# A two-layer graph network kernel: counting ahead of the messages, a second accumulator for the visits of the last four groups, and a ring of eight gathered quads

## The chip, the cores and the metric

The kernel runs on one core of a Trainium2 chip. The metric is the device time of one execution in microseconds (us). The engines are named as in the profile: PE is TensorE (PEld its weight load), DVE VectorE, ACT ScalarE, POOL GpSimd, SP SyncE.

## What is computed

There are 6,250 nodes with 128 features and 200,000 directed edges, sorted by target (`dst`). Both layers use the same edges; only the first uses the edges' 128 features.

```python
# layer 0, for each edge
m   = silu(concat(x[src], x[dst], e) @ msg_W1 + msg_b1) @ msg_W2 + msg_b2
agg = segment_sum(m, dst)
x1  = layernorm(x + layernorm0(x + mlp2(concat(x, agg))))
# layer 1
agg = segment_sum(x1[src], dst) / max(degree, 1)
out = layernorm(x1 + relu(relu(concat(x1, agg) @ W1 + b1) @ W2 + b2))
```

## The kernel before

**Units of work.** 128 edges are a tile, 4 tiles a quad (512 edges), 7 quads a group. There are 391 quads with edges in 56 groups (0 to 55), and the nodes are 49 blocks of 128. The edge stage is a loop over steps `s`; in each, every engine does its part of quad `s` or of a neighbour.

**The messages of layer 0.** POOL gathers the rows of the sources, four indirect DMAs a quad (L899), into a ring of nine quads (`gath`, `GS = 9`). Before those of quad `s` it waits until DVE's addition for quad `s - 9` is done. PE computes `ps_pre` (`products`, L1200 and L1207) for quad `s + 1`. DVE adds the gathered rows (`add`, L979, waits for `pre_mm`, `silu` and the gather). ACT applies silu (L1419). PE then sums over edges into the group's window of targets (`sums`, L1241 and L1243), for which it waits for `silu`. DVE adds a finished group's window to the accumulator `sumT` in SBUF (`add_sums`, L987).

**The counts for layer 1.** Layer 1's sum over sources needs, for each group, a matrix of how often each node is the source of each target of the group. It is counted by PE from one-hots of the edges. For quad `s + 1`, in step `s`, DVE makes the one-hots (`hots`: four of L964 and four of L966), PE multiplies them (`count`, eight of L1221 and two of L1227 that carry a column over), and in the next step ACT copies the counts out (`copy_counts`, L1363 and L1368). The integer keys of a group come from DVE (`make_keys`), and the finished matrix of a group goes to HBM in four parts (`store`, L1389) in the steps after its last quad. So counting runs one quad ahead of the sums and ends with them, in step 390.

**Visits.** Nodes' features after layer 0 (`x1`) are finished in 17 units of 2 to 4 blocks, as the sorted targets allow (`UNITS`, `unit_step`). A unit takes steps `s0` to `s0 + 9`, one small stage on one engine in most of them; the last one (blocks 46 to 48) starts at step 392, since it needs all messages. A visit `(s, d, lo, hi)` multiplies blocks `lo` to `hi` of `x1` with group `d`'s count matrix, which SP has loaded back (`load_visits`, L785), two matmuls for a block (L1257); DVE adds the 120 columns of the result to `sumT` (`add_visits`, L1012) one step later. `plan_visits` gives each step up to two visits of together at most 14 blocks (a bucket), four after step 391. A group can be visited from step `7(d + 1) + 9` on, since its matrix must be in HBM. Visits add to the same `sumT` as the messages' sums, whose columns are zeroed when their unit has been read (L1051), so a group whose window is not yet zeroed cannot be visited: groups 52 to 55 wait for the last unit. PE has two banks for visits, used in turn by buckets; a bucket waits until DVE has added the one before last.

**The tail.** From step 392 the last unit goes through its ten steps, the visits that are left are made, and 13 last units `w` (four blocks each) go through layer 1's update: POOL scales by the degree (L908), PE (L1317, L1319), ACT, PE (L1327, L1329), DVE, ACT, store. They follow the visits in an order set by `plan_last`.

PE in a step of before:

```python
products(s + 1); unit_step(s); visit(i) for i in VISITS_AT.get(s, ())
last_step(...); sums(s); count(s + 1)
```

## Time and profile before

| | us |
|---|---|
| median of 3 timed runs | 2902.84 (2895.51 to 2920.19) |
| profiled execution, its own time | 2885.56 |
| its span, first to last instruction | 2883.7 |
| first addition for a quad (step 0) to the last (step 390) | 85 to 2746.9 |
| from the last unit's first matmul to the end | 2753.25 to 2883.7 |

All busy times, stages and waits below are of the one profiled execution. The span is 1.9 us shorter than its time, and that time is 17.3 us below the median of the timed runs.

### The profile page before, as it was taken

How to read it: one execution, taken by the hardware profiler on the slowest of the kernel's cores; microseconds unless marked ns; L12 is line 12 of the kernel's file. 1: busy time of each engine (PE TensorE's matmuls, PEld its weight loads, DVE VectorE, ACT ScalarE, POOL GpSimd, SP SyncE). 2: the span in 40 equal slices, each digit the busy share in tenths (PEclk: the TensorE clock that was granted, in tenths of full speed). 3: DMA queues.
4: the chain of work that ended last, by engine and by line, in shares of the span. 5: the costliest groups of instructions: out<-in, count | busy, mean ns of one | idle time of the engine just before them, and what ended most of it. 6: DMA issues, size and time to landing. Idle time of an engine off the chain costs nothing.

```text
span 2883.7 us, 58406 instructions
## 1 busy us (share of the span) xinstructions
PE 2275.3 (79%) x19559; PEld 1944.8 (67%) x19559; DVE 1681.2 (58%) x5671; ACT 1475.2 (51%) x3771; POOL 1518.6 (53%) x1633
## 2 busy tenths in 40 slices
PE   5778777878787888777777778878888788887986
PEld 4666666666676766666666667767677676776874
DVE  5465655665555565565565656566555556555735
ACT  3454554555464554454555555455555454554614
POOL 5555556556555555555555555455554555554322
PEclk7776777877777876887888888888888888898998
DMA  6454555554555564555565555666565666666683
GB/s 218 121 153 142 148 152 152 160 150 150 162 155 154 153 175 142 177 166 169 152 182 164 174 173 176 185 167 182 165 187 173 174 193 173 186 173 192 200 296 97
DMA packets 305361, 487.72 MB, mean 169 GB/s; under 512 B 121342, under 2 KB 183944, under 8 KB 305056
## 3 DMA queue, kind: packets, MB, share of 16 engines
q10 hardware_dynamic: 94161, 245.05, 26.0%
q1 hardware_dynamic: 158895, 129.93, 16.4%
q0 software_dynamic: 52000, 108.96, 14.4%
q8 instruction: 158, 2.59, 0.4%
q14 instruction: 147, 1.20, 0.1%
HBM read 375.62 MB, written 108.13 MB: 168 GB/s over the span
## 4 chain that ended last, share of the span: by engine, by line
PE 48%; another core or an unknown queue 15%; issue 14%; DVE 10%; ACT 9%; ACTq 3%; DMA 1%; DVEq 0%; SPq 0%
PE ps_pre L1200 12%; PE ps_cnt L1221 11%; PE ps_l L1257 9%; PE ps_sum L1241 8%; DVE edgeK L966 4%; ACT counts L1363 3%; PE ps_pre L1207 3%; ACT farN L1399 2%; DVE edgeL L964 2%; ACT h L1419 1%; ACTq L1496 1%; PE ps_sum L1243 1%; DVE pre L979 1%; DVE nodeE L956 1%
## 5 line engine op out<-in xcount | busy, mean ns | idle before, releaser
L899 POOL DMA_INDIRECT gath<-P_d,src_i x1527 | 1444.3, 946 | 1185.4 <-DVE pre L979 748.0
L1200 PE MATMUL ps_pre<-wc,eT_c 128*128 128x128 f32 x3128 | 730.2, 354 | 61.7 <-issue 59.7
L1221 PE MATMUL ps_cnt<-edgeK,edgeL 128*128 128x250 bf16 (+1 forms) x3128 | 578.0, 338 | 197.8 <-ACT counts L1363 110.1
L1200 PEld LDWEIGHTS ps_pre<-wc,eT_c 128*128 128x128 f32 x3128 | 593.3, 234 | 119.6 <-issue 84.5
L966 DVE TENSOR_SCALAR edgeK<-iotaK,key 128x500 bf16<-128x500 f16 (+1 forms) x1564 | 667.7, 488 | 0.0
L979 DVE TENSOR_TENSOR pre<-ps_pre,gath 128x512 f32<-128x512 f32 x384 | 262.9, 685 | 686.5 <-remote 462.9
L1363 ACT ACTIVATE counts<-ps_cnt 128x1000 bf16<-128x1000 f32 x391 | 405.5, 1037 | 414.9 <-remote 228.2
L1241 PE MATMUL ps_sum<-edgeN,h 128*128 128x40 f32 x3128 | 481.5, 302 | 80.6 <-issue 68.9
L1221 PEld LDWEIGHTS ps_cnt<-edgeK,edgeL 128*128 128x128 bf16 x3128 | 319.0, 111 | 309.9 <-issue 210.3
L1241 PEld LDWEIGHTS ps_sum<-edgeN,h 128*128 128x128 f32 x3128 | 448.7, 217 | 101.2 <-issue 79.8
L1257 PE MATMUL ps_l<-A_v,x1h 128*128 128x120 bf16 x5020 | 359.7, 229 | 85.6 <-issue 74.6
L1207 PE MATMUL ps_pre<-Qw,nodeE 120*128 120x128 bf16 x1564 | 385.3, 246 | 38.9 <-issue 29.1
L1409 ACT ACTIVATE edgeN<-farN 128x160 f32<-128x160 f32 x391 | 127.9, 327 | 525.1 <-remote 435.0
L1399 ACT ACTIVATE farN<-iotaN,rel_g 128x40 f32<-128x40 f16 x1564 | 380.6, 314 | 29.9 <-issue 29.6
L1257 PEld LDWEIGHTS ps_l<-A_v,x1h 128*128 128x128 f16 x5020 | 315.3, 105 | 116.1 <-issue 101.1
L1419 ACT ACTIVATE h<-pre 128x512 f32<-128x512 f32 x391 | 243.2, 622 | 191.4 <-DVE pre L979 155.1
L964 DVE TENSOR_SCALAR edgeL<-iotaL,low 128x132 bf16<-128x132 f16 x1564 | 328.4, 272 | 0.0
L1012 DVE TENSOR_TENSOR sumT<-ps_l,sumT 128x120 f32 x443 | 123.6, 279 | 228.4 <-remote 154.6
L1207 PEld LDWEIGHTS ps_pre<-Qw,nodeE 120*128 120x128 bf16 x1564 | 181.2, 116 | 43.5 <-issue 33.7
L1243 PEld LDWEIGHTS ps_sum<-edgeB,onesb 128*128 128x128 bf16 x1564 | 118.3, 127 | 62.7 <-issue 62.7
L1243 PE MATMUL ps_sum<-edgeB,onesb 128*128 128x40 bf16 x1564 | 117.0, 188 | 52.3 <-issue 52.2
L956 DVE TENSOR_SCALAR nodeE<-rel_c,pidq 120x512 bf16<-120x512 bf16 x391 | 134.7, 345 | 2.4 <-DMA rel_c<-rel_d 2.4
(184 smaller groups left out, 1425.0 us busy)
## 6 DMA issues: line engine op xcount, KB each, us to landing
eT_c<-eT ACTq DMA_DIRECT2D x193, 512.0 KB
A_d<-counts ACTq DMA_DIRECT2D x168, 384.0 KB
rel_c<-rel_d ACTq DMA_DIRECT2D x193, 240.0 KB
A_v<-A_d SPq DMA_DIRECT2D x68, 448.0 KB
A_v<-A_d SPq DMA_DIRECT2D x97, 256.0 KB
gath<-P_d,src_i POOLq DMA_INDIRECT x1535
A_d<-counts ACTq DMA_DIRECT2D x56, 416.0 KB
A_v<-A_d SPq DMA_DIRECT2D x33, 384.0 KB
```

Of the source, the lines that this page charges most:

```text
L899: pool.indirect_dma_start(gath[:, r, t * D:(t + 1) * D], None, v["P_d"], bass.IndirectOffsetOnAxis(ap=src_i[g % RS][:, c:c + 1], axis=0)). ...
L964: V.tensor_scalar(edgeL[x][:, j, :], iotaL[:, :, 0:LC], low[k][:, q * QT + j:q * QT + j + 1], None, ALU.is_equal)
L966: last = V.tensor_scalar(edgeK[x][:, ROFF[j]:ROFF[j] + A2 * w], iotaK[j][:, :, 0:A2 * w // KR], key[k][:, q * QT + j:q * QT + j + 1], None ...
L979: V.tensor_tensor(pre[s % 2][:], ps_pre[s % 2][:], gath[:, s % GS, :], ALU.add).then_inc(pre_add, 1)
L1200: T.matmul(o, eT_c[c % RE][:, e0:e0 + P], wc[:], start=True, stop=False)
L1207: last = T.matmul(o, nodeE[x][:, t * P:(t + 1) * P], Qw[g % 2][:, q, :], start=False, stop=True)
L1221: last = T.matmul(o[:, :, w0:w0 + w], edgeL[x][:, j, 0:P], r, start=(j == 0), stop=(j == QT - 1 and q == 0), skip_group_check=True)
L1241: T.matmul(ps_sum[:, cols], h[x][:, t, :], edgeN[x][:, t, :], start=False, stop=True, skip_group_check=True)
L1257: last = T.matmul(l1_part(i), x1h[:, a, part, :], A[:, (a - lo) * P:(a - lo) * P + GW], start=(a == lo and part == 0), stop=(a == hi - 1 a ...
L1363: A.activation(counts[k][:].rearrange("p (b a) d -> p b a d", b=2)[:, :, :, bass.ds(off, W0)], ps_cnt[:, :, 0:AB * W0].rearrange("p b (a d ...
L1399: last = A.activation(farN[:, j, :], iotaN[:, q, :, 0:WN // KR], ACT.Square, scale=-1.0, bias=rel_g[k][:, q * QT + j:q * QT + j + 1])
L1419: A.activation(h[x][:, :, 0:D], pre[x][:].rearrange("p (t n) -> p t n", n=D), ACT.Silu).then_inc(silu, 1)
```

## The change

**Counting ahead** (`plan_counts`). The counts have a schedule of their own. `COUNT_AT[s]` is the quad counted at the end of step `s`, as before. In 42 steps (12, 18, 24 and so on to 258) there is an extra count (`EXTRA_AT[s]`), placed on PE between the products and the sums. So the count runs 43 quads ahead of the messages from step 258 on, and its last one is made in step 347. On DVE the one-hots for an extra count of step `s` are made at the end of step `s - 1`'s; on ACT, in such a step, the copy of the earlier count goes ahead of silu, and that of the extra one behind it. Steps 348 to 390 hold no counting.

**What goes with it.** Keys for counting are made from arrays of their own (`src_c`, `dst_c`, `first_c`), which SP loads with three small DMAs a group; ACT's distances wait for a subtraction of its own on DVE (`relate`) instead of `keyed`. The parts of a finished matrix are stored two a step, and `STORED` gives the step from which a group can be visited.

**Visits.** Times of visits are half steps `t`. From step 355 to 391 a step can hold two buckets of up to three visits and 14 blocks each, the second between the sums and the next step's products. SP may load them into twelve slots from step 355 on instead of four (these include the buffers of the one-hots and of the counts, which are free by then).

**The second accumulator.** Visits of groups 52 to 55 made before the last unit is zeroed go to `sum2` (536 columns, zeroed at step 7), which is added to `sumT` once, right behind the zeroing.

| blocks visited in steps | before | after |
|---|---|---|
| 0 to 347 | 1770 | 1814 |
| 348 to 391 | 518 | 762 |
| from 392 | 456 | 168 |
| visits, all steps | 443 | 525 |

**The ring** has eight quads (`GS = 8`).

```diff
-GS, RS = 9, 3
+GS, RS = 8, 3
+EARLY, EVERY, FIRST_EXTRA = 42, 6, 12
+def plan_counts():
+
+    main, extra, c, s = {}, {}, 1, 0
+    while c < NQ:
+        if s >= FIRST_EXTRA and s % EVERY == 0 and c - s - 1 < EARLY:
+            extra[s], c = c, c + 1
+        if c < NQ:
+            main[s], c = c, c + 1
+        s += 1
...
+        if second and not COUNTED + LEAD <= s < QUADS:
...
-                if s < (d + 1) * GQ + GQ + 2 or zeroed < NB and 112 * d + SLACK + GW > P * zeroed:
+                if s < STORED[d] + LEAD + 1 or zeroed < NB and d < D2 and 112 * d + SLACK + GW > P * zeroed:
...
+                to = sum2[:, bass.ds(base - O2, GW)] if i in ASIDE else sumT[:, bass.ds(base, GW)]
+                V.tensor_tensor(to, l1_part(i), to, ALU.add).then_inc(changed, 1)
...
+                if u == len(UNITS) - 1:
+                    dve.wait_ge(changed, CHANGE["merge"] - 1)
+                    V.tensor_tensor(sumT[:, O2:O2 + W2], sum2[:], sumT[:, O2:O2 + W2], ALU.add).then_inc(changed, 1)
```

In a step of PE:

```diff
+                if s in EXTRA_AT:
+                    count(EXTRA_AT[s])
                 if s < NQ:
                     sums(s)
-                if s + 1 < NQ:
-                    count(s + 1)
+                for i in VISITS_AT.get(2 * s + 1, ()):
+                    visit(i)
+                if s in COUNT_AT:
+                    count(COUNT_AT[s])
```

In a step of DVE:

```diff
-                if s + 1 < NQ:
-                    if q == GQ - 1:
-                        dve.wait_ge(prepared, g + 2)
-                    hots(s + 1)
+                for c in (COUNT_AT.get(s), EXTRA_AT.get(s + 1)):
+                    if c is not None:
+                        if c % GQ == 0:
+                            dve.wait_ge(prepared, c // GQ + 1)
+                        hots(c)
```

In a step of ACT:

```diff
+                made = 0 if s == 0 else COUNT_AT.get(s - 1)
+                if s + 1 < NQ:
+                    distances(s + 1)
+                if s in EXTRA_AT:
+                    copy_next(made)
                 if s < NQ:
                     activate(s)
                     load_chunk_of(s)
...
+                if s in EXTRA_AT:
+                    copy_next(EXTRA_AT[s])
+                elif made is not None:
+                    copy_next(made)
```

On PE, step 12, the first with an extra count (`ps_pre` is the products, `ps_sum` the sums, `ps_cnt` the count). Before:

```order
L1200 MATMUL ps_pre<-wc,eT_c 128x128
L1207 MATMUL ps_pre<-Qw,nodeE 128x128
L1241 MATMUL ps_sum<-edgeN,h 128x40 x4
L1243 MATMUL ps_sum<-edgeB,onesb 128x40 x4
L1221 MATMUL ps_cnt<-edgeK,edgeL 128x25x10 x2
L1221 MATMUL ps_cnt<-edgeK,edgeL 128x25x12 x2
L1221 MATMUL ps_cnt<-edgeK,edgeL 128x25x10 x2
L1221 MATMUL ps_cnt<-edgeK,edgeL 128x25x12 x2
L1227 MATMUL ps_cnt<-carry,identb 128x25 x2
```

After:

```order
L1281 MATMUL ps_pre<-Qw,nodeE 128x128
L1295 MATMUL ps_cnt<-edgeK,edgeL 128x25x10 x2
L1295 MATMUL ps_cnt<-edgeK,edgeL 128x25x12 x2
L1295 MATMUL ps_cnt<-edgeK,edgeL 128x25x10 x2
L1295 MATMUL ps_cnt<-edgeK,edgeL 128x25x12 x2
L1301 MATMUL ps_cnt<-carry,identb 128x25 x2
L1315 MATMUL ps_sum<-edgeN,h 128x40 x4
L1317 MATMUL ps_sum<-edgeB,onesb 128x40 x4
L1295 MATMUL ps_cnt<-edgeK,edgeL 128x25x10 x2
L1295 MATMUL ps_cnt<-edgeK,edgeL 128x25x12 x2
L1295 MATMUL ps_cnt<-edgeK,edgeL 128x25x10 x2
L1295 MATMUL ps_cnt<-edgeK,edgeL 128x25x12 x2
```

One count more stands between products and sums; the one behind the sums is of a first quad of a group here and has no carry.

On PE, the last unit's stages (`ps_u`) with the visits (`ps_l`) that stand between them; L1290 and L1301 are its fourth and its last stage. Before:

```order
L1257 MATMUL ps_l<-A_v,x1h 128x120 x56
L1290 MATMUL ps_u<-bias,onesb 128x384
L1292 MATMUL ps_u<-ident,xT_u 128x128 x3
L1257 MATMUL ps_l<-A_v,x1h 128x120 x140
L1301 MATMUL ps_u<-ident,x_u 128x128 x3
L1257 MATMUL ps_l<-edgeK,x1h 128x120 x56
L1257 MATMUL ps_l<-counts,x1h 128x120 x156
L1257 MATMUL ps_l<-A_v,x1h 128x120 x52
```

After (`ps_pre<-gath,l_w` is the first of the last units):

```order
L1358 MATMUL ps_u<-ident,xT_u 128x128
L1364 MATMUL ps_u<-bias,onesb 128x384
L1366 MATMUL ps_u<-ident,xT_u 128x128 x3
L1375 MATMUL ps_u<-ident,x_u 128x128 x3
L1331 MATMUL ps_l<-counts,x1h 128x120 x24
L1331 MATMUL ps_l<-A_v,x1h 128x120 x96
L1391 MATMUL ps_pre<-gath,l_w 128x512
L1393 MATMUL ps_pre<-sumT,l_w 128x512
```

No visit stands between the unit's stages any more, and the first of the 13 last units follows after 120 matmuls of visits.

## Rows read from the trace of the kernel before

**Rows 1.** The page's part 2: granted clock of TensorE in 40 slices, in tenths

```profile
PEclk7776777877777876887888888888888888898998
```

**Rows 2.** Busy time by stretch: us of each engine (instructions), clock, DMA share, GB/s

```profile
163.30:1820.30 1657.00, 1310.90 (x10438) 1114.91 (x10437) 979.06 (x3291) 874.11 (x2285) 931.13 (x984) 0.79 0.54 161
2463.00:2703.50 240.50, 196.09 (x1937) 169.44 (x1936) 140.14 (x488) 130.65 (x325) 125.06 (x132) 0.87 0.63 181
2703.50:2746.90 43.40, 42.25 (x519) 39.51 (x519) 36.27 (x109) 29.85 (x81) 2.83 (x3) 1.00 0.70 220
2753.00:2780.00 27.00, 19.52 (x274) 17.67 (x272) 8.91 (x40) 4.71 (x9) 6.38 (x10) 0.87 0.90 310
```

**Rows 3.** The same for the tile ps_pre alone: PE's products, DVE's additions, one a step

```profile
163.30:1820.30 1657.00, 490.96 (x2953) 407.90 (x2952) 168.47 (x246) 0.00 (x0) 0.79 0.54 161
2463.00:2703.50 240.50, 62.14 (x396) 49.65 (x396) 22.53 (x33) 0.00 (x0) 0.87 0.63 181
2703.50:2746.90 43.40, 13.67 (x108) 11.59 (x108) 6.17 (x10) 0.00 (x0) 1.00 0.70 220
```

**Rows 4.** Waits, steps 12 to 258: us in total, times, longest

```profile
POOL gath L899 <- DVE pre L979: 451.8, 163, 9.0
ACT edgeN L1409 <- remote: 250.8, 59, 7.3
PE ps_cnt L1221 <- ACT counts L1363: 97.3, 49, 6.7
```

**Rows 5.** Groups, steps 12 to 258: POOL's gathers, DVE's one-hots, by form

```profile
L899 POOL DMA_INDIRECT gath<-P_d,src_i x984 | 931.1, 946 | 725.0 <-DVE pre L979 451.8 <-issue 273.2
L966 DVE TENSOR_SCALAR edgeK<-iotaK,key 128x600 bf16<-128x600 f16 x492 | 232.9, 514 | 0.0
L966 DVE TENSOR_SCALAR edgeK<-iotaK,key 128x500 bf16<-128x500 f16 x492 | 207.2, 462 | 0.0
L964 DVE TENSOR_SCALAR edgeL<-iotaL,low 128x132 bf16<-128x132 f16 x984 | 206.6, 271 | 0.0
```

**Rows 6.** Busy time by stretch for the tile ps_cnt alone: PE's counts

```profile
163.30:1820.30 1657.00, 391.43 (x2390) 257.80 (x2390) 0.00 (x0) 255.80 (x246) 0.79 0.54 161
2703.50:2746.90 43.40, 10.64 (x88) 7.99 (x88) 0.00 (x0) 9.36 (x9) 1.00 0.70 220
```

**Rows 7.** Busy time of two stretches: all engines, the tile pre, the tile ps_l

```profile
85.00:629.00 544.00, 426.59 (x3090) 360.71 (x3089) 323.51 (x1076) 289.51 (x768) 317.15 (x336) 0.77 0.50 145
85.00:629.00 544.00, 0.00 (x0) 0.00 (x0) 57.34 (x84) 52.23 (x84) 0.77 0.50 145
85.00:629.00 544.00, 12.96 (x138) 10.36 (x139) 3.94 (x14) 2.99 (x5) 0.77 0.50 145
2170.00:2376.00 206.00, 169.68 (x1631) 146.76 (x1629) 118.74 (x408) 101.98 (x259) 105.99 (x113) 0.85 0.62 181
2170.00:2376.00 206.00, 0.00 (x0) 0.00 (x0) 19.40 (x29) 17.47 (x28) 0.85 0.62 181
2170.00:2376.00 206.00, 48.15 (x648) 41.97 (x649) 12.79 (x46) 0.00 (x0) 0.85 0.62 181
```

**Rows 8.** Timeline of PE and DVE in the tail: start, us, what [idle before]

```profile
2753.25 0.91 PE L1271 MATMUL ps_u<-sumT,wagg 128*128 128x384 f32 x2
2771.72 7.44 PE L1257 MATMUL ps_l<-A_v,x1h 128*128 128x120 bf16 x112 [6.62 <-DMA A_v<-A_d]
2779.33 3.10 PE L1257 MATMUL ps_l<-edgeK,x1h 128*128 128x120 bf16 x56
2791.68 1.53 DVE L1012 TENSOR_TENSOR sumT<-ps_l,sumT 128x120 f32 x4 [0.32 <-DVE sumT L1012]
2843.55 0.37 PE L1257 MATMUL ps_l<-edgeK,x1h 128*128 128x120 bf16 x4 [2.34 <-DVE sumT L1012]
2854.76 0.39 PE L1327 MATMUL ps_cnt<-bias,onesb 65*128 65x512 bf16 x1 [0.78 <-ACT pre L1468]
2858.54 0.39 PE L1327 MATMUL ps_cnt<-bias,onesb 65*128 65x512 bf16 x1 [0.78 <-ACT pre L1468]
```

More of the change, by code:

```diff
@@ L48 @@
 KQ = 3 * WN
+D2 = 52
 CQ, RE = 2, 3
@@ L122, in plan_last @@
         start[s] = now
-        blocks = sum(VISITS[i][3] - VISITS[i][2] for i in VISITS_AT.get(s, ()))
-        now += max(0.1 * blocks, 0.3 * len(VISITS_AT.get(s, ())), 1.5 if s <= QUADS + U_LEN else 0.7)
+        blocks = sum(VISITS[i][3] - VISITS[i][2] for i in VISITS_AT.get(2 * s, ()))
+        now += max(0.1 * blocks, 0.3 * len(VISITS_AT.get(2 * s, ())), 1.5 if s <= QUADS + U_LEN else 0.7)
     steps, first = [], 0
     for w in range(len(LAST_UNITS)):
-        first = max(first, start[VISITS[LAST_VISIT[w]][0] + 1] + 2)
+        first = max(first, start[VISITS[LAST_VISIT[w]][0] // 2 + 1] + 2)
         steps += [(next(s for s in start if start[s] >= first + t), first + t, w, k) for k, t in enumerate(L_STEPS)]
@@ L155, in plan_slots @@
             at += hi - lo
-        pieces[s] = parts
+        pieces[t] = parts
         count[r] += len(parts)
-        landed[s] = 16 * count[r]
+        landed[t] = 16 * count[r]
     return slot, before, offset, pieces, landed
@@ L203, in changes_of_sums @@
             at["zero", UNIT_AT[s][0]] = n
+            if UNIT_AT[s][0] == len(UNITS) - 1:
+                n += 1
+                at["merge"] = n
+        for i in VISITS_AT[ADDED_LATE[s]] if s in ADDED_LATE else ():
+            n += 1
+            at["visit", i] = n
     return at
 CHANGE = changes_of_sums()
+ASIDE = {i for i, (t, d, lo, hi) in enumerate(VISITS) if d >= D2 and CHANGE["visit", i] < CHANGE["merge"]}
 def bass_gnn_two_layers(nc, x_nm, xT, eT, src_pt, dst_pt, src_row, dst_row, dst_first, dst_last,
@@ L684, in build_edges @@
     first_i = [v["first_i0"], sb("first_i1", [P, GT], I32)]
+    src_c, dst_c, first_c = ([sb(f"{n}_c{k}", [P, GT], I32) for k in range(2)] for n in ("src", "dst", "first"))
     nodeE = [sb(f"nodeE{k}", [KQ, QT * P], BF16) for k in range(2)]
@@ L719, in build_edges @@
     onehots = sem("onehots")
+    related = sem("related")
+    c_in = [sem(f"c_in{k}") for k in range(2)]
     keyed, far, near = sem("keyed"), sem("far"), sem("near")
@@ L839, in fast @@
                     load_ids(g + 1)
+                for c in range(GQ + 1, NQ, GQ):
+                    if COUNT_STEP[c] == s and c // GQ + 1 < GROUPS:
+                        load_count_ids(c // GQ + 1)
                 unit_loads(s)
@@ L1027, in split_biases @@
         def split_biases(s):
+            if s == GQ:
+                V.memset(sum2[:], 0.0)
             if s == 2 * GQ:
```

164 lines of the change are left out of this document (98 added, 66 removed).

## The prediction

> **What bounds the kernel now.** I read the page first: the granted clock is 0.7 to 0.8 in most slices, so PE is at 1.2 GHz for some 40% of the time [rows 1]. Then the busy times by stretch with the number of additions in each (one a step). Steps 12 to 258 take 1657.0 us for 246 steps, 6.74 us each; steps 348 to 381 take 240.5 us for 33, 7.29 each; the last 9 take 43.4 us, 4.82 each [rows 2, 3]. In these last ones POOL has no more gathers to issue (2.83 us of work against 125.06), and PE is full (42.25 of 43.4 us) at 2.4 GHz. In the others PE is busy for 79 to 82% of the time, more than any other engine: 1310.9 / 246 = 5.33 us of 6.74.
>
> The waits tell what it is not. POOL stands 451.8 us before its gathers because the ring has no free quad [rows 4]: the gathers are a whole ring ahead, and DVE's addition waits for PE, not for them. POOL's four gathers take 4 x 0.946 us, with the 273.2 us of issue gaps spread over 246 steps 4.9 us a step [rows 5]. That is a floor under PE's 6.74. ACT's waits of up to 7.3 us whose releaser is unknown ("remote", 59 times) are for PE's sums [rows 4]; there PE itself makes no headway, and the rows do not say why. So the edge stage goes at PE's pace, with some idle time in it in which a little more work might fit.
>
> The tail lasts from 2753.25 to 2883.7 us, 130.4 us. PE works through the last unit with visits between its stages, then stands 6.62 us for the matrices' loads at a DMA share of 0.90 and 310 GB/s, ends the visits only at 2843.9 us, and then makes one last unit every 3.78 us (2854.76 to 2858.54) [rows 2, 8].
>
> **Part 1, the extra counts of steps 12 to 258.** 42 counts are added there. A count is 1.59 us of PE (391.43 / 246) at this clock, and 1.18 us (10.64 / 9) at 2.4 GHz [rows 6]. What does a piece of PE work cost in such a step? Two stretches tell. From 85 to 629 us there are 84 steps of 6.48 us with 1.4 matmuls of visits each (138 less 20 transposes that share the tile); from 2170 to 2376 us there are 28 of 7.36 us with 23.1 [rows 7]. So 21.7 matmuls cost 0.88 us, 0.041 us each, where back to back at 2.4 GHz they take 0.055 us (3.10 us / 56) [rows 8]. The ratio is 0.74: part of what is added fills idle time, and the granted clock goes from 0.77 to 0.85. For a count that gives 0.74 x 1.18 = 0.87 to 0.74 x 1.59 = 1.18 us. I take 0.95 us, near the lower one, for the same rows show the clock rising with the work: **+40 us**. The bounds are 0.5 us (most of it hidden in PE's idle 1.4 us a step), +21, and 1.9 us (all of its 1.59 and the wait for ACT's copy, 97.3 / 246 = 0.4, less a little), +80.
>
> The trace shows the granted clock at 0.77 with 5.1 us of PE work a step and at 1.00 where PE is full [rows 2, 7]. The Trainium skill, TensorE: Matmul & The Clock Gate, "What's actually happening", says the throttled state is the default and activity releases it. By that rule a count added to a thin step costs less than its busy time; without it the sum would have 1.59 us for each, +67.
>
> On the other engines the extra work has room on average. A set of one-hots is 4 x 0.271 + 2 x 0.514 + 2 x 0.462 = 3.04 us of DVE [rows 5], which is busy for 979.06 / 246 = 3.98 us of 6.74 [rows 2]; the step before an extra count then has 7.0 us of DVE work. ACT gets a copy and a carry more, 255.8 / 246 = 1.04 us and a small carry [rows 6], on top of 3.55. The extra keys, loads of ids (three of 14 KB a group) and subtractions are moved or small. I cost them at nothing; should a PE step wait for the one-hots of an extra count, it is rival 3.
>
> The gathers' rows show 946 ns whatever DVE does beside them, and POOL idle for 725.0 us [rows 5]. The Trainium skill, SBUF — State Buffer, "Who interferes with whom", says that a DVE operation in a two-port mode and GpSimd exclude each other for a whole instruction. By it the 42 x 3.04 = 128 us of one-hots could hold the gathers back, which speaks against this change; POOL's idle time would take it in, and the sum would stay.
>
> **Part 2, steps 348 to 390.** 43 counts go. 34 of them are in steps with gathers, at 0.95 us, and 9 in full steps at 1.18 us: 32 + 11 = 43 us. Into these steps and the one after come 762 - 518 = 244 blocks, 488 matmuls at 0.041 us: 20 us. Net **-23 us**. The bounds: -48 with each count at 1.59 us, and +5 if the visits' handling takes over the room. A step of then holds up to six visits, which on DVE are 6 x 0.38 us (four in 1.53 us [rows 8]), 2.3 us with their register loads beside, in place of 3.04 us of one-hots. DMA: stores of 224 KB a step stop and 180 KB of loads come, so the 181 GB/s stay.
>
> **Part 3, the ring.** The last gather is issued eight steps before the end and not nine, so one step moves from 4.82 to 7.29 us: **+2 us**. Otherwise the ring has slack, as POOL's wait for it shows. Bounds 0 and +4.
>
> **Part 4, the tail.** 456 blocks become 168. The last unit has no visits between its stages. Of its 27 us (2753 to 2780) the 6.62 us of load wait and nearly all visit matmuls go; what is left is some 13 us of passing from engine to engine. Then 5 buckets of four visits at DVE's pace of 1.53 + 0.32 = 1.85 us, 9 us; then 9 buckets (24 matmuls, 1.4 us of PE) with some four last units of 3.4 us (3.78 less the 0.78 idle, and a bit of start) between them, 26 us; then eight last units at 3.78 us, 30 us; and the run-out as now: 2854.76 is unit 8's second product, four more at 3.78 us leave 14 us to the end, 16 with the first product. Together 94 to 97 us against 130.4: **-34 us**. Bounds: -48 if the last units keep 3.78 us from the start, -22 if PE's clock drops in the thin unit chain and the visits end later.
>
> The zeroing and the merge of `sum2` are two operations of about half a microsecond.
>
> **The sum.** 40 - 23 + 2 - 34 = **-15 us**. On the profiled execution's own 2885.6 us that is 2870.6. The timed runs' median lies 17.3 us above it, and I carry the difference over: 2902.8 - 15 = **2888 us**. Seen from above: the PE work is the same in total, and only the tail's idle time and the ratio of 0.74 pay for what is gained.
>
> **Rivals.**
>
> Rival 2, the early counts ride free (faster). The steps without gathers take 4.82 us with a full PE and those with them 6.7 to 7.3 us with a PE at 80%; something that goes with the gathers adds time that is not PE work. If an added count falls into it, part 1 is +8 us instead of 40. Against it: the 0.74 was measured in just such steps. Then 2902.8 - 47 = 2856 us.
>
> Rival 3, the extra steps cost more than the count (slower). The place is the step before and with an extra count: DVE makes two sets of one-hots in a row, 6.1 us, ahead of the addition of the next quad, and ACT copies a count and its carry, over 1 us, ahead of silu. PE has the last count, the products and the extra count to do meanwhile, 1.2 + 13.67 / 9 = 1.5 + 1.2 us at full clock [rows 3, 6], against 3.04 us, 0.7 for the addition and about as much for silu. Where PE's part is under that 4.4 us, DVE's decides. If they do in most of the 42 steps the price is 2.3 us each, +97 instead of +40: 2902.8 + 42 = 2945 us. For it speak the 97.3 us that PE already waits for ACT's copies; against it, that at 1.2 GHz PE's part is 6 us.
>
> Rival 4, the late steps gain nothing. Six small visits a step, each handed from PE to DVE over two banks, and loads in pieces of 64 KB take the place of the one-hots; part 2 is +5. Then 2902.8 + 13 = 2916 us.
>
> **How the numbers follow.** Chances: forecast 0.45, rival 2 0.25, rival 3 0.15, rival 4 0.15. A measurement of this kernel tells about 1% (29 us) from no change; the three runs of before lie 25 us apart. Faster by over 1% takes 0.28 of the forecast's chance (its own spread is some 25 us) and 0.85 of rival 2's: 0.34. Slower by over 1% takes 0.04 of the forecast's, 0.8 of rival 3's and 0.2 of rival 4's: 0.17. Within 1%: 0.49. The bounds of all four parts together are -75 and +61 us with all at one end; the range leaves out the outer part of rivals 2 and 3: 2846 to 2928.
>
> **What would show it right or wrong.** Right: steps 12 to 258 take 1690 to 1705 us instead of 1657 with a granted clock above 0.79, and 43 steps from 348 on take some 261 us instead of 284. PE has no wait for loads in the last unit, x1's last transposition comes about 13 us after the unit's first matmul, and the tail is 94 to 97 us. POOL goes on waiting for DVE before its gathers. Rival 2: the early steps stay at 1657 to 1670 us. Rival 3: DVE's addition or ACT's silu in steps 12, 18, ... starts late, PE waits for silu there, and the early steps take over 1730 us. Rival 4: PE waits for `changed` or for the loads in steps 355 to 391. The forecast is wrong altogether if the time lost where PE makes no headway changes with the counts' place, since its cause is unknown.

## The result, and the profile after

The changed kernel takes 2973.41 us (median of 4 runs, 2963.78 to 2993.28), the kernel before 2911.52 us on the same chip (4 runs, 2895.51 to 2931.67). The ratio is 1.0235, with a 95% interval of 1.0191 to 1.0279: **2.3% slower**, where 0.5% faster was forecast. Its profiled execution took 2980.81 us, 2979.0 of them the span.

The stages, cut at the same additions as before:

| stage | before, us | after, us | difference | forecast |
|---|---|---|---|---|
| steps 12 to 258 | 1657.0 | 1763.6 | +106.6 | +40 |
| steps 258 to 348 | 642.7 | 643.7 | +1 | 0 |
| steps 348 to 390 | 283.9 | 291.9 | +8 | -23 + 2 |
| last unit's first matmul to the end | 130.5 | 111.0 | -19.5 | -34 |

Busy time by stretch, after: steps 12 to 258, 348 to 381 and 381 to 390. The columns are those of [rows 2]: PE, PEld, DVE, ACT, POOL (instructions), granted clock, DMA share, GB/s.

```profile
164.40:1928.00 1763.60, 1330.45 (x10820) 1134.35 (x10818) 1085.74 (x3673) 916.80 (x2357) 929.15 (x984) 0.80 0.53 157
2571.70:2820.40 248.70, 199.78 (x2189) 183.39 (x2187) 77.00 (x257) 93.17 (x270) 124.73 (x132) 0.83 0.67 194
2820.40:2863.60 43.20, 38.13 (x431) 35.75 (x430) 22.90 (x74) 17.70 (x59) 6.59 (x7) 0.89 0.48 139
```

Beside [rows 2], PE is busy for only 19.6 us more in the first stretch (1310.90 to 1330.45), which is 106.6 us longer. So 87.0 us of the loss, most of it, is time in which PE stands by its record. The same stretches for the tile ps_cnt (the first) and the tile ps_l (the second):

```profile
164.40:1928.00 1763.60, 435.14 (x2781) 295.04 (x2782) 0.00 (x0) 299.17 (x287) 0.80 0.53 157
...
2571.70:2820.40 248.70, 100.73 (x1320) 85.12 (x1317) 35.35 (x125) 0.00 (x0) 0.83 0.67 194
```

The counts alone went up by 43.7 us against [rows 6], about 1.0 us for each of the 42. From step 348 the counts are gone (PE spent 46.95 us on 34 of them before) and visits have taken their place, 54.64 us before.

Waits, after, steps 12 to 258; total, times, longest:

```profile
POOL gath L958 <- DVE pre L1040: 579.7, 177, 10.1
...
ACT counts L1441 <- remote: 238.0, 65, 9.3
ACT edgeN L1487 <- remote: 214.9, 56, 7.4
PE ps_cnt L1295 <- ACT counts L1441: 163.0, 70, 8.4
...
DVE edgeL L1025 <- remote: 124.2, 29, 7.7
...
ACT counts L1441 <- PE ps_cnt L1301: 98.1, 69, 4.1
```

Two lines answer to [rows 4]: PE waits 163.0 us for ACT's copies instead of 97.3, and POOL waits longer still for a free quad, so the gathers and the shorter ring are not what is late. New is DVE's wait ahead of its one-hots (edgeL), 124.2 us where it had none; but DVE's idle time as a whole is the same (1657.0 - 979.06 and 1763.6 - 1085.74 us, 677.9 each), so this wait has only changed its place.

What such a wait looks like: the timeline of PE, then of ACT and DVE, in step 252, which has an extra count. Columns: start, us of work, engine, line, what, and in brackets the idle time before it and what ended it.

```profile
1885.69 1.14 PE L1295 MATMUL ps_cnt<-edgeK,edgeL 128*128 128x250 bf16 x8
1886.67 0.21 PE L1301 MATMUL ps_cnt<-carry,identb 128*128 128x25 bf16 x2
...
1887.29 1.08 PE L1315 MATMUL ps_sum<-edgeN,h 128*128 128x40 f32 x8
1888.21 0.27 PE L1317 MATMUL ps_sum<-edgeB,onesb 128*128 128x40 bf16 x4
1896.09 1.12 PE L1295 MATMUL ps_cnt<-edgeK,edgeL 128*128 128x250 bf16 x4 [7.62 <-ACT counts L1441]
```

```profile
1894.94 1.01 ACT L1441 ACTIVATE counts<-ps_cnt 128x1000 f32 x1 [7.46 <-remote]
...
1894.94 0.85 DVE L1025 TENSOR_SCALAR edgeL<-iotaL,low 128x132 bf16<-128x132 f16 x4 [6.49 <-remote]
```

PE's record has the extra count done at 1886.88 us. ACT and DVE both wait for it and both start at 1894.94, 8 us later. PE may not begin the main count before ACT has copied the extra one, so it stands 7.62 us, although the copy itself takes 1.01. I call such a stretch, several us long, between the recorded end of PE's work and the news of it a **stop**. What goes on in it is open. The trace keeps the semaphore events of PE's work, the signals that its waiters start on. In step 252 those of the count and of the sums come at 1894.92 and 1895.05 us, 0.13 us apart, while PE's record has the two ends 1.6 us apart. News held back fits this as well as a PE that makes no headway.

Idle time of PE right ahead of the main count, steps 12 to 258 (247 steps):

| | before, us | after, us |
|---|---|---|
| all steps | 134.8 | 235.2 |
| gaps of over 3 us | 53.0 (11 gaps) | 139.3 (28 gaps) |
| of these in the 42 extra steps | 0 | 75.5 (14 gaps) |

The kernel before has stops too: ahead of all 11 of its long gaps the event of the count comes 4.8 to 9.8 us after the recorded end. After, it comes 3.0 to 8.4 us late in the 26 of 28 cases in which the trace kept the event. But before, the next count is a whole step away from the last one. These gaps grew by 100.4 us and PE's idle time in the stretch by 87.0, so idle time elsewhere fell by 13.

The times from one addition of DVE (`add`) to the next, steps 12 to 258, show two delays and not one. Mean us, before and after: up to the addition of an extra step 6.75 and 9.17, to the next one 6.52 and 4.56, to the one behind that 6.45 and 9.34, and the other three steps together 20.68 and 19.94. The first delay, 2.4 us, is where DVE has made two sets of one-hots in a row; PE goes on meanwhile, and 2.0 us of it are made up at once. The second, 2.9 us, lies behind the gap ahead of the main count and is not made up in the next step.

The tail. PE in the last unit, and two of the last units:

```profile
2868.03 1.65 PE L1345 MATMUL ps_u<-sumT,wagg 128*128 128x384 f32 x2 [1.89 <-DVE deg L1049]
...
2878.60 0.50 PE L1364 MATMUL ps_u<-bias,onesb 65*128 65x384 bf16 x1 [2.04 <-DVE z_u L1134]
...
2884.50 0.90 PE L1375 MATMUL ps_u<-ident,x_u 128*128 128x128 f32 x3 [4.12 <-ACT x_u L1523]
...
2926.49 0.61 PE L1401 MATMUL ps_cnt<-bias,onesb 65*128 65x512 bf16 x1 [3.40 <-ACT pre L1544]
...
2933.00 0.39 PE L1401 MATMUL ps_cnt<-bias,onesb 65*128 65x512 bf16 x1 [0.78 <-ACT pre L1544]
...
2940.50 0.61 PE L1401 MATMUL ps_cnt<-bias,onesb 65*128 65x512 bf16 x1 [4.50 <-ACT pre L1544]
```

The load wait of [rows 8] is gone and the unit has only its own chain left, but PE goes through it at 1.2 GHz (granted clock 0.50 from 2868 to 2886 us): the first product takes 1.65 us for the 0.91 of [rows 8], and the transposition comes 16.5 us after it. Two last units begin after 3.40 and 4.50 us instead of 0.78. Together 111.0 us, not 94 to 97.

### The profile page after: what moved, and what is told of

It is laid out like the page before. It is cut to its first block, busy times and chain, and to the rows that moved or that the text cites. A ratio compares the mean times of both kernels' runs of the same rounds, so it can differ in the third digit from the quotient of the medians.

```text
span 2979.0 us, 58840 instructions
## 1 busy us (share of the span) xinstructions
PE 2261.5 (76%) x19559; PEld 1938.4 (65%) x19559; DVE 1712.0 (57%) x5755; ACT 1466.7 (49%) x3771; POOL 1516.0 (51%) x1633
## 3 DMA queue, kind: packets, MB, share of 16 engines
q1 hardware_dynamic: 192975, 132.31, 16.5%
## 4 chain that ended last, share of the span: by engine, by line
PE 53%; issue 14%; another core or an unknown queue 13%; ACT 10%; DVE 6%; ACTq 3%; DMA 1%; DVEq 0%; SPq 0%; POOL 0%; POOLq 0%
PE ps_pre L1274 13%; PE ps_cnt L1295 12%; PE ps_l L1331 10%; PE ps_sum L1315 8%; ACT counts L1441 4%; PE ps_pre L1281 3%; ACT farN L1477 2%; DVE edgeK L1027 2%; ACT h L1495 1%; ACTq L1568 1%; PE ps_sum L1317 1%; DVE edgeL L1025 1%; DVE pre L1040 1%; ACT edgeN L1487 1%
## 5 line engine op out<-in xcount | busy, mean ns | idle before, releaser
L1295 PE MATMUL ps_cnt<-edgeK,edgeL 128*128 128x250 bf16 (+1 forms) x3128 | 566.0, 334 | 294.5 <-ACT counts L1441 187.4
L1315 PE MATMUL ps_sum<-edgeN,h 128*128 128x40 f32 x3128 | 465.7, 297 | 63.0 <-issue 57.2
L1315 PEld LDWEIGHTS ps_sum<-edgeN,h 128*128 128x128 f32 x3128 | 433.9, 211 | 81.7 <-issue 65.5
L1025 DVE TENSOR_SCALAR edgeL<-iotaL,low 128x132 bf16<-128x132 f16 x1564 | 328.7, 272 | 160.5 <-remote 124.2
L1331 PE MATMUL ps_l<-A_v,x1h 128*128 128x120 bf16 x4416 | 316.4, 227 | 86.5 <-issue 83.9
L1331 PEld LDWEIGHTS ps_l<-A_v,x1h 128*128 128x128 f16 x4416 | 275.1, 104 | 110.0 <-issue 104.5
L1076 DVE TENSOR_TENSOR sumT<-ps_l,sumT 128x120 f32 x505 | 140.2, 278 | 236.0 <-PE ps_l L1331 99.1
```

Source lines behind the costliest of these rows:

```text
L1025: V.tensor_scalar(edgeL[x][:, j, :], iotaL[:, :, 0:LC], low[k][:, q * QT + j:q * QT + j + 1], None, ALU.is_equal)
L1295: last = T.matmul(o[:, :, w0:w0 + w], edgeL[x][:, j, 0:P], r, start=(j == 0), stop=(j == QT - 1 and q == 0), skip_group_check=True)
L1315: T.matmul(ps_sum[:, cols], h[x][:, t, :], edgeN[x][:, t, :], start=False, stop=True, skip_group_check=True)
L1331: last = T.matmul(l1_part(i), x1h[:, a, part, :], A[:, (a - lo) * P:(a - lo) * P + GW], start=(a == lo and part == 0), stop=(a == hi - 1 a ...
```

## The experiments

The 18 runs fell on chips of two kinds. On three chips the kernel before takes 2906 to 2915 us, as in the result; on two it takes 2133 and 2135 us. That was not chosen, and it turned out to be the most telling thing of all. Every time is a median, every ratio is to the kernel before on the same chip, stage times are of the profiled execution.

### First chip (before: 2135.27 us)

No extra counts:

```diff
-EARLY, EVERY, FIRST_EXTRA = 42, 6, 12
+EARLY, EVERY, FIRST_EXTRA = 0, 6, 12
```

> The changed kernel with no count ahead (EARLY = 0): the counts go at the old rhythm, the split keys, the ring of eight, the half steps and the second accumulator stay. In the changed kernel steps 12 to 258 took 1763.6 us against 1657.0 before. Theory (the extra counts are the whole loss there): 1650 to 1670 us here, and the whole kernel at 0.995 to 1.01 of the one before. Rival (the split keys, the extra small DMAs or the ring cost it): 1700 us or more.

2131.24 us, ratio 0.9983 (0.9973 to 0.9994); steps 12 to 258 1211.6 us, tail 120.8. The ratio lies where the theory had it, but the stage can't be set beside its 1650 to 1670 us, for here every step is shorter.

Seven of an extra count's eight one-hots left out:

```diff
-            for j in range(QT):
+            for j in range(0 if s in THIN else QT):
...
-            for j, (w0, w) in enumerate(WIN):
+            for j, (w0, w) in list(enumerate(WIN))[3 if s in THIN else 0:]:
```

> The changed kernel; of the eight one-hot operations of each of the 42 extra counts DVE makes only the last (the other seven are left out, the counts of those quads are not the reference's). Theory A (two sets of one-hots in a row hold up the next addition, then silu, the copy and the second count): steps 12 to 258 fall from 1763.6 to 1680 to 1710 us. Theory B (the second count waits for the copy of the first on ACT, since there is one ps_cnt): within 15 us of 1763.6. Theory C (PE's own work): no change either.

2116.20 us, 0.9912 (0.9882 to 0.9941); steps 12 to 258 1220.9 us.

ACT copies 40 of the 1000 columns of an extra count:

```diff
-            A.activation(counts[k][:].rearrange("p (b a) d -> p b a d", b=2)[:, :, :, bass.ds(off, W0)],
-                         ps_cnt[:, :, 0:AB * W0].rearrange("p b (a d) -> p b a d", d=W0),
+            nb, na = (1, 2) if s in THIN else (2, AB)
+            A.activation(counts[k][:].rearrange("p (b a) d -> p b a d", b=2)[:, 0:nb, 0:na, bass.ds(off, W0)],
+                         ps_cnt[:, 0:nb, 0:na * W0].rearrange("p b (a d) -> p b a d", d=W0),
```

> The changed kernel; ACT's copy of each extra count takes 40 columns of 1000 (the rest is left out, the counts of those quads are not the reference's), so that 42 operations of 1.04 us become 42 of some 0.3. Theory B (waits for ACT's copies): steps 12 to 258 fall by 30 to 60 us from 1763.6. Theories A and C: by under 12 us.

2113.85 us, 0.9908 (0.9881 to 0.9936); steps 12 to 258 1216.6 us.

PE does two of the eight matmuls of an extra count, and its carries:

```diff
-                for j, (w0, w) in enumerate(WIN):
+                for j, (w0, w) in list(enumerate(WIN))[0:1 if s in THIN else QT]:
...
```

> The changed kernel; PE makes 2 of the 8 matmuls of one-hots of each extra count and its two carries (6 are left out, the counts are not the reference's). Theory C (PE's own work is the cost, 1.6 us a count): steps 12 to 258 fall by 40 to 50 us from 1763.6. Theories A and B: by under 20 us, for the waits stay.

2114.49 us, 0.9898 (0.9870 to 0.9926); steps 12 to 258 1220.1 us.

The three thinned ones agree with each other within their intervals, and with the unthinned kernel on the second chip (0.9913, next section): nothing that is taken out of an extra count gives time back here. These runs could not tell the theories apart, because what they were to explain was not there.

### Second chip (before: 2132.97 us)

The changed kernel; the same with ACT's copy of the extra count right behind silu; and the kernel before with the ring alone:

```diff
             A.activation(h[x][:, :, 0:D], pre[x][:].rearrange("p (t n) -> p t n", n=D), ACT.Silu).then_inc(silu, 1)
+            if s in EXTRA_AT:
+                between()
             if s + 1 < NQ:
                 equals(s + 1)
...
```

```diff
-GS, RS = 9, 3
+GS, RS = 8, 3
```

> The changed kernel itself, once more. On the chip of the runs with the thinned counts the kernel before took 2135 us and not 2911, a step 4.9 us and not 6.7, POOL waited for nothing and PE had no outages. Theory P (the extra counts cost time only where PE's headway is broken by outages): on such a chip steps 12 to 258 take 1210 to 1225 us, as without counts ahead (1211.6), and the whole is 0.985 to 0.995 of before. Theory A/B (two counts in a step cost by themselves, about 2.5 us each): 1300 us or more and the whole 1.03 of before. On a chip with outages (a step of 6.7 us before): 1.02 again.

> The changed kernel; in the 42 steps with an extra count ACT copies it right behind silu, ahead of the two operations that make the next edgeN and edgeB (0.64 us). Theory B (the second count waits for the copy): faster than the changed kernel by up to 0.6 us in each of the 42 steps, 25 us, on a chip with outages; nothing on one without. Theory A (one-hots): no difference.

> The kernel before with a ring of eight gathered quads. By the prediction 1.001 of before (one more step with gathers). Rival: on a chip where DVE's addition waits for the gathers (228 us in the run without counts ahead) the shorter ring costs more, 1.005 to 1.01.

Changed: 2115.49 us, **0.9913 (0.9893 to 0.9934)**, faster. Copy first: 2113.62 us, 0.9906 (0.9884 to 0.9928), no different. Ring alone: 2138.35 us, 1.0028 (1.0015 to 1.0041), some 6 us, over the +2 of part 3.

Steps 12 to 258, all engines and then ps_cnt; first the kernel before with a ring of eight:

```profile
122.90:1341.10 1218.20, 1105.38 (x10485) 981.91 (x10485) 972.50 (x3293) 866.98 (x2287) 921.96 (x972) 0.91 0.74 218
...
122.90:1341.10 1218.20, 329.03 (x2400) 234.30 (x2400) 0.00 (x0) 256.14 (x247) 0.91 0.74 218
```

and the changed kernel, with its first waits:

```profile
127.20:1348.70 1221.50, 1099.70 (x10835) 978.27 (x10835) 1076.57 (x3673) 903.36 (x2357) 924.89 (x974) 0.96 0.76 226
...
127.20:1348.70 1221.50, 358.87 (x2789) 263.96 (x2788) 0.00 (x0) 297.98 (x287) 0.96 0.76 226
```

```profile
POOL gath L958 <- issue: 289.9, 951, 0.3
ACT counts L1441 <- issue: 78.8, 92, 1.9
PE ps_cnt L1295 <- ACT counts L1441: 62.4, 99, 2.2
```

POOL has no idle time left but its own issue gaps: 974 gathers and 289.9 us make 1214.8 of the 1221.5 us. Here a step is four gathers, 4.95 us, the floor that the prediction worked out, and PE comes along. The longest wait for a copy is 2.2 us instead of 8.4; no gap between sums and count is over 3 us: there are no stops. The stage is 3.3 us longer with the 42 extra counts than in the kernel before with a ring of eight, and the clock rises from 0.91 to 0.96. The delay behind the double set of one-hots is here too (7.05 us instead of 5.15 up to the addition of an extra step), and is wholly made up: six steps take 29.79 us, and 29.71 in the ring-of-eight kernel. Steps 348 to 390 gain 7 us (214.0 to 206.7), the tail 21 (130.6 to 109.6). This is rival 2's case. But these chips differ from the others in two things at once: there are no stops, and POOL sets the pace instead of PE. The fillings of the next section were to part the two and fell on a chip with stops, so no run shows a full PE without them.

### Third chip (before: 2915.05 us)

Two ways to fill PE, in the kernel before with a ring of eight and in the changed one: 25 fp32 matmuls ahead of every fifth product, or 5 ahead of each. What they write is overwritten.

```diff
+                for _ in range(25 * (s % 5 == 1) if t == 0 and 12 < s < 258 else 0):
+                    T.matmul(o, eT_c[c % RE][:, e0:e0 + P], wc[:], start=True, stop=True)
                 T.matmul(o, eT_c[c % RE][:, e0:e0 + P], wc[:], start=True, stop=False)
```

```diff
-                for _ in range(25 * (s % 5 == 1) if t == 0 and 12 < s < 258 else 0):
+                for _ in range(5 if t == 0 and 12 < s < 258 else 0):
```

> The kernel before with a ring of eight, and with 25 extra fp32 matmuls in a row (they write the first of a quad's products once more, and are overwritten by it) ahead of every fifth product between steps 12 and 258: 49 holes made by hand, in which PE does nothing for the step. One such matmul has 0.20 us of busy time (617.3 us over 3128 in the ring-of-eight run), so a hole is about 5 us, as long as the recorded ones, and 1.0 us a step in the mean; PE had 0.45 us a step to spare (1102 busy of 1214 us). All theories: steps 12 to 258 go from 1218 to some 1350 to 1420 us. This is the base for the next run.

> The changed kernel with the same 49 holes. Theory A (holes are what makes an extra count dear: the second count of a step waits for the copy of the first and for a second set of one-hots, and PE gets no lead with which to make a hole good): steps 12 to 258 are over 85 us longer than in the kernel before with holes, over 2 us for each of the 42 extra counts, and over 15 gaps between sums and count are over 3 us. Theory B (PE is simply the bound there and a count costs its own PE time, 1.33 us by 328 us over 246 steps): 40 to 65 us longer. Theory C (the extra counts still ride free, and the recorded loss has another cause than holes): under 15 us longer.

> The kernel before with a ring of eight and the same number of extra matmuls spread evenly, 5 ahead of each product between steps 12 and 258: PE's work is the same as with the holes and there are no holes. All theories: steps 12 to 258 between 1320 and 1400 us, no more than with the holes. This is the base for the next run.

> The changed kernel with 5 extra matmuls ahead of each product. Theory A (holes are what makes an extra count dear): here, without holes, the 42 counts cost no more than their own PE time, 40 to 65 us over the kernel before with the same filling, and clearly less than the changed kernel loses with the holes. Theory B (the count's own PE time): the same 40 to 65 us as with the holes. Theory D (the copy and the second set of one-hots make an extra count dear as soon as PE is the bound, holes or none): over 85 us here too.

| | median, us | ratio | steps 12 to 258 | gaps between sums and count, us |
|---|---|---|---|---|
| old, holes | 3090.31 | 1.0609 (1.0548 to 1.0671) | 1837.6 | 90.6 |
| changed, holes | 3132.40 | 1.0752 (1.0709 to 1.0796) | 1900.7 | 174.5 |
| old, even | 2962.32 | 1.0171 (1.0135 to 1.0206) | 1707.6 | 25.5 |
| changed, even | 3042.43 | 1.0430 (1.0392 to 1.0468) | 1820.1 | 117.2 |

The old kernel goes outside what all theories gave for the holes (up to 1420): on this chip their base is 1657 and not the 1218 us that the expectation started from. Theory A fell: with the holes made by hand the changed kernel is 63.1 us longer in the stage, 1.5 for each extra count (B's price), and without them 112.5 us, 2.7 each. Theory D (over 85 us, holes or none) is met without the holes and missed with them. By the ratios the loss is 1.4% with the holes and 2.6% without; the unfilled kernel's 2.2 to 2.4% is not clear of the second. The holes do bring A's long gaps (20 of over 3 us against 8), but not its price. So holes of one's own making did not make the extra counts dearer, as theory A had it.

Even filling, steps 12 to 258, all engines; the kernel before, then the changed one:

```profile
165.30:1872.90 1707.60, 1454.24 (x12875) 1304.58 (x12872) 981.68 (x3292) 875.81 (x2281) 933.47 (x984) 0.90 0.53 156
```

```profile
168.40:1988.50 1820.10, 1508.73 (x13270) 1349.01 (x13268) 1089.20 (x3673) 918.47 (x2357) 929.68 (x984) 0.89 0.51 152
```

With the clock at 0.90 and 0.89, PE's own work for the 42 counts is plain: 54.5 us, 1.30 each. The other 58 us are idle. The waits of the same stretch, the kernel before and then the changed one:

```profile
PE ps_cnt L1223 <- ACT counts L1365: 14.9, 29, 0.9
```

```profile
DVE edgeL L1025 <- remote: 153.4, 34, 7.8
...
PE ps_cnt L1297 <- ACT counts L1443: 68.9, 43, 7.6
```

With a full PE the kernel before never stands over 0.9 us for a copy. The changed one does, up to 7.6 us, and all of its 9 gaps of more than 3 us ahead of the main count (51.0 us) are in steps with an extra count. One of them:

```profile
1162.42 0.21 PE L1303 MATMUL ps_cnt<-carry,identb 128*128 128x25 bf16 x2
...
1164.47 0.18 PE L1319 MATMUL ps_sum<-edgeB,onesb 128*128 128x40 bf16 x1 [0.48 <-issue]
...
1169.57 1.17 ACT L1443 ACTIVATE counts<-ps_cnt 128x1000 f32 x1 [8.87 <-remote]
```

Again the copy begins 6.9 us after the recorded end of the extra count, with ACT idle for 8.87 us.

### Fourth chip (before: 2912.21 us)

The even filling with one part of the extra count thinned or moved at a time (the edits of the first two chips), and the change without extra counts and without filling.

> The changed kernel with the even filling of z4_new_even, in which DVE makes only the last of the eight one-hots of an extra count (the other seven are left out, so the counts are wrong data for the same PE and ACT work). If the second set of one-hots is what costs (5 us of DVE work ahead of the next addition), steps 12 to 258 fall from 1820 to under 1765 us on a chip like that one; if it is the copy or the stops, they stay over 1790 us. Where the kernel before takes about 2135 us: 1220 to 1400 us, and the run tells only that a full PE alone doesn't make the counts dear.

> The same filling; ACT copies 40 of the 1000 columns of an extra count, so that the copy takes some 0.2 us instead of 1.04 (the rest of that count's data is left out). If the length of the copy between the two counts is what costs, steps 12 to 258 fall by some 35 us (42 times 0.85) to about 1785 us; if it is when ACT and DVE hear of the first count at all, by under 15 us.

> The same filling, nothing left out; ACT copies the extra count right behind silu, ahead of the comparisons of the next step (1.6 us of work) instead of behind them. If ACT's order is what costs, steps 12 to 258 fall by 30 to 65 us (0.7 to 1.6 us for each extra count); if the stops are, ACT stood idle ahead of the copy in the long gaps anyway, and they fall by under 20 us.

> The changed kernel with no extra counts and no filling: ring of eight, second accumulator and more visits in the late steps remain. On a chip where the kernel before takes about 2910 us every theory that blames the extra counts expects steps 12 to 258 at 1650 to 1670 us as before, the last steps a few us longer for the count and the visits that stay, the tail 5 to 15 us shorter, and a ratio of 0.993 to 1.003. If the ring or the second accumulator were to blame, it would be over 1.01. Where the kernel before takes 2135 us: a ratio of 0.997 to 1.000, as once before.

| | median, us | ratio | steps 12 to 258 |
|---|---|---|---|
| one-hots thinned | 2993.41 | 1.0271 (1.0213 to 1.0329) | 1771.2 |
| copy thinned | 3029.71 | 1.0397 (1.0305 to 1.0488) | 1812.0 |
| copy first | 3052.09 | 1.0481 (1.0423 to 1.0539) | 1814.1 |
| no extra counts, no filling | 2912.75 | 1.0014 (0.9979 to 1.0048) | 1678.2 |

Against 1820.1 us (and a ratio of 1.0430 on the third chip) the thin one-hots give 49 us in the stage and 1.6% of the time; the stage lies between the two thresholds that were set (1765 and 1790), near the one for the one-hots. Of the 58 us that PE stood idle more they take away 40, and of the nine long gaps five are left (26.2 us). Thinning the copy of the extra count gives 8 us in the stage, and making it earlier 6: neither its length nor its place is the matter, as the idle ACT ahead of it says. (The expectation for the place counts 1.6 us of work; what the copy passes is edgeN and edgeB, 0.64 us, so 27 us was the most it could give.) PE's 54 us, the one-hots' 49 and the copy's 8 come to the 112 us that the filled kernel loses, if they add up, which single profiled executions on two chips can't show. And the last row is the plain undoing: **without the extra counts the change is as fast as the kernel before**. Its steps 12 to 258 take 1678.2 us, 8 more than the 1650 to 1670 that were expected, on an execution of 2919.64 us. Its steps 348 to 390 take 294.5 us, 10.6 more than in the profile of before, its tail 120.5, 10 less.

### Fifth chip (before: 2906.35 us)

The one-hots again, without filling: thinned; or with nothing left out and the four of edgeK made one step later, behind the addition; and the changed kernel beside them.

```diff
+                if s in EXTRA_AT:
+                    hots(EXTRA_AT[s], 1)
                 for c in (COUNT_AT.get(s), EXTRA_AT.get(s + 1)):
...
-                        hots(c)
+                        hots(c, 0 if c == EXTRA_AT.get(s + 1) else None)
```

> The changed kernel without filling; DVE makes only the last of the eight one-hots of an extra count (seven left out). Where the kernel before takes about 2910 us: if the one-hots make half of the loss, as with the filling, steps 12 to 258 fall from 1764 to 1700 to 1730 us and the time from 2973 to 2915 to 2945 us. If the filling had made them dear, they stay over 1745 us.

> The changed kernel with nothing left out; of an extra count's one-hots DVE makes the four of edgeL (0.84 us) where it made all, and the four of edgeK (1.7 us) one step later, behind the addition of the messages. If their place ahead of that addition is what costs, most of what leaving them out gives comes back: steps 12 to 258 under 1740 us. If DVE's work itself costs, wherever it stands, or PE now waits for them ahead of the extra count, they stay over 1750 us.

> The changed kernel itself, beside the other two on their chip. Where the kernel before takes about 2910 us: steps 12 to 258 at 1750 to 1780 us and a ratio of 1.019 to 1.028; where it takes about 2135 us: a ratio of 0.989 to 0.994.

| | median, us | ratio | steps 12 to 258 | gaps between sums and count, us |
|---|---|---|---|---|
| one-hots thinned | 2963.78 | 1.0224 (1.0146 to 1.0302) | 1726.9 | 188.4 |
| one-hots split | 2972.25 | 1.0213 (1.0124 to 1.0302) | 1746.2 | 143.4 |
| changed | 2964.94 | 1.0223 (1.0147 to 1.0299) | 1767.9 | 236.5 |

The changed kernel repeats its loss on another chip, in size (1.0223) and place (+110.9 us in steps 12 to 258 against the profile of before, gaps 236.5 us). The other two disagree with themselves: their stages are 41 and 22 us shorter in the profiled execution, but the medians show nothing. (The split one's 1746.2 us also lies between its two thresholds, 1740 and 1750.) The profiled execution of the thinned kernel was the fastest of its four (2957.67 us) and that of the changed one the slowest of its five (2986.42), and the intervals are 0.8% wide on either side. So without filling the share of the one-hots stays **open**. One thing can be read from the split one:

```profile
165.30:1911.50 1746.20, 1363.69 (x10821) 1154.29 (x10821) 1084.64 (x3674) 917.14 (x2362) 930.93 (x985) 0.79 0.54 159
```

Its gaps ahead of the main count are back at 143.4 us, near the 134.8 of before, yet it gets only a fifth of the 110.9 us back: PE's busy time is 1363.69 us instead of 1328.85, for the same matmuls; a matmul of the sums (ps_sum<-edgeN,h) takes 308 ns in the mean instead of 299, for more of them run at 1.2 GHz. In this pair of executions the wait taken away is partly paid back as PE's busy time.

## Why the prediction was wrong

**Part 1, +40, measured +107: the step that failed.** "What does a piece of PE work cost in such a step?" was answered with a ratio of 0.74, taken from stretches with more and fewer visits [rows 7], and used for counts. A visit's matmuls stand alone: PE does them whenever it has time, and only a later addition wants them. An extra count is a link, by the kernel's order: the main count of the same step needs the one PSUM tile that ACT must first empty, and DVE's next one-hots need the buffer that the count has read. So it puts a second hand-over PE to ACT to PE into one step. When a stop falls between the two, PE has only the sums to go on with (1.4 us in step 252) and stands for the rest; the trace has 14 such gaps, 75.5 us, where before had none. The upper bound had this as "the wait for ACT's copy, 97.3 / 246 = 0.4" a count: a mean over steps with one count each, which says nothing of steps with two. And the second set of one-hots was costed "at nothing". In their place the runs showed 2.54 us for each extra count between the two profiled executions, of which 1.0 is the count's own busy time. The medians give less: the extra counts make 1.0235 out of 1.0014, 64 us, and what the changed kernel takes less than the run without them from step 348 on is 12 us, so an estimate from these is 76 / 42 = 1.8 us each, still about twice the 0.95. That the extra counts are the loss is shown by leaving them out; that a stop between two counts is what makes them dear is argued from where the gaps lie, for no run took the stops away and left PE full.

The gathers were not held back by the longer one-hot work: 944 ns each (929.15 / 984) instead of 946.

**Rival 3** had this price, 2.3 us each, and the steps (12, 18, ...), and it is what happened in size. Of its signs, DVE's addition does start late in these steps (9.17 us for 6.75) and the stage is over 1730 us; a wait of PE for silu there is not seen (PE stands 6.2 us in all ahead of and within the sums of these steps, 14.4 before). Its double set of one-hots is a large part of the loss when PE is full (49 of 112.5 us in the stage, 1.6 of 2.6% by the ratios) and not shown when it is not. Its copy ahead of silu was not tested: the two runs on the copy (8 and 6 us) touch the copy of the extra count, which stands behind silu. What it did not have is the stop ahead of the copy, although "its cause is unknown" stood in the prediction and named the place where the forecast would break.

**Rival 2** is right on the chips without stops, where POOL sets the pace: there the early counts cost 3.3 us together, and the whole change is 0.9% faster. Against it I had held that the 0.74 was measured in just such steps, which is the same failed step once more.

**Part 2, -23, measured with part 3's step +8: rival 4's size.** Its sign was not seen: from 2627 to 2820 us PE has no wait for `changed` or for loads of over 1.3 us in all. Both rates were off. Taking 34 counts away took 45.8 us from PE (46.95 to 1.19), but the 547 visit matmuls that came took 46.1 us (54.64 to 100.73), 0.084 us each, where the forecast had 0.041 us of time for one. PE's busy time stays where it was (196.09 to 199.78 us) while the clock falls from 0.87 to 0.83. In the last nine steps PE went from full to 38.13 us of 43.2 and nothing was gained: there POOL is done and PE waits. The run without extra counts keeps its counts in these steps and takes 294.5 us for them, so what their going gave, with the visits that came for them, is about 3 us, from single executions on two chips.

**Part 3, +2.** The ring alone costs 0.28% (0.15 to 0.41%), 6 us, on a chip whose steps go at POOL's pace. Small, as said, if a little over its bound of 4.

**Part 4, -34, measured -19.5 (-21 on the second chip).** The mechanism is right: no load waits, no visits in the last unit, shorter. The size is below the lower bound (-22), for the reason that this bound named and the forecast did not use: the clock. The thin chain of the last unit runs at 1.2 GHz, 16.5 us instead of "some 13 us of passing", and PE falls back to 1.2 GHz in the last units, where it then stands 3.40 and 4.50 us instead of 0.78. On the second chip the tail is 109.6 us, so this does not come from the stops.

The sum: between the two profiled executions the misses are 67 us in part 1, 29 in parts 2 and 3 and 14 in part 4, which make the forecast's -15 the +95.3 that the spans show (2883.7 to 2979.0). The medians differ by 61.9 us only: the profiled execution of before (2885.6 us) was 26 us below its median, that of after 7 above. So a third of the stages' 95 us is scatter of the two executions, wherever that lies. By the medians the whole of the loss hangs on the extra counts: without them the ratio is 1.0014. The bounds were also added wrongly: 80 + 5 + 4 - 22 is +67 us and not +61.

## What to carry to other kernels

Before a marginal price is taken from one kind of work and used for another, ask whether the new piece stands alone or is a link in a hand-over; a second PE to ACT to PE hand-over in one step can cost what the slowest hand-over of the trace costs, not its mean (14 of 42 extra counts here). When an extra piece needs work on another engine, price that too, and not at nothing because the engine has room on average. Long waits whose releaser the profile can't name are a condition of the machine that a change can walk into: price a change that shortens the distance between two dependent pieces with those waits, and keep both outcomes apart in the chances. A change can be 0.9% faster on one chip and 2.3% slower on another, so one chip's verdict should carry its time of the kernel before with it.

## What the runs showed of the hardware

The same kernel before takes 2133 and 2135 us on two chips, and 2906 to 2915 us on three and in the result: 36% between them, and each kind repeats within 0.4%. On the faster chips a step is four gathers of POOL, 4.95 us, the clock 0.91 to 0.96, and no gap between sums and count is over 3 us but one of 3.1. On the slower ones it is 6.7 us at a clock of 0.79. About every fourth step of the kernel before (59 of 246) ACT waits there for a releaser that the profile does not name, 4.3 us in the mean and 7.3 at most, and the events of PE's work come 3 to 10 us after the recorded end wherever it then stands for over 3 us ahead of a count. The traces of these chips also lack more semaphore events: 319 of the 391 of the counts are kept in the kernel before, all 391 on the second chip with a ring of eight; so some waits may have no named releaser for that reason alone. The cause of the stops stays open; no run made them come or go. They are not seen to go with PE's fetching of instructions: in the kernel before the gaps of over 3 us end 5 to 27 us after the last of the 16 KB packets that its queue (by their number PE's) fetches every 18 us in the mean.

The one thing that weakened their effect was more work. With five matmuls more ahead of each product PE's busy time in steps 12 to 258 grew by 143 us (1310.90 to 1454.24) and the stage by only 51 (the kernel before with a ring of eight lost 1.7%). The clock rose from 0.79 to 0.90, PE's idle time fell from 346 to 253 us, and the gaps between sums and count fell from 134.8 to 25.5 us. The same matmuls in lumps of 25 cost 6.1%.

On the slower chips no version was faster than the kernel before. On the faster ones the changed kernel and the one with the copy first are, by 0.9% each, and without extra counts it is 0.2%.
